# A graph network on one core: blocks of 2500 edges in the sorted last layer, layer norms with a bias on ScalarE, and loads moved into a prelude

## What is computed

```python
h = relu(layernorm(x));  x = x + gcn(h)         # msg = norm[row] * norm[col] * h[col], segment sum, @ W.T + b
h = relu(layernorm(x));  x = x + gat(h)         # 4 heads, softmax over each destination's edges
h = relu(layernorm(x));  x = x + weighted(h)    # two weighted steps: sum of x[src] * ew, mean, two matmuls, leaky relu
h = relu(layernorm(x))                          # last layer, edge-conditioned:
xw = h @ W                                      # 3125 x 128
ew = edge_attr @ edge_w                         # 103125 x 16 @ 16 x 128
msg = xw[src] * ew
out = segment_sum(msg, dst, num_segments=3125) + b
x = x + out
```

## Time and profile before

| | |
|---|---|
| median of three runs | 2925.09 us |
| profiled execution, its own time | 2937.53 us |
| its span, mean granted clock | 2935.8 us, 0.902 |
| PE / PEld busy | 2349.3 (80%) / 1710.9 (58%) |
| DVE / ACT / POOL busy | 1910.0 (65%) / 1408.7 (48%) / 1953.1 (67%) |
| hardware DMA queue | 171548 packets, 246.53 MB |
| software DMA queue (POOL's) | 48720 packets, 36.84 MB |

### The profile page before, as it was taken

The page is one execution under the profiler, slowest core; times in us unless marked ns, Lnnn a source line. Parts: engine busy times, 40 slices in busy tenths (PEclk is TensorE's granted clock), DMA queues, the critical chain, the costliest instruction groups (busy, mean ns, idle before and its releaser), DMA issues. The chain is left out here.

```text
span 2935.8 us, 64938 instructions
## 1 busy us (share of the span) xinstructions
PE 2349.3 (80%) x22192; PEld 1710.9 (58%) x22192; DVE 1910.0 (65%) x3810; ACT 1408.7 (48%) x2659; POOL 1953.1 (67%) x1608
## 2 busy tenths in 40 slices
PE   4677777766857777777788787889978999999998
PEld 2466666663424555555555555434546777777777
DVE  7999999983457777777777787211134555556555
ACT  0498988880038777777777775000003221222211
POOL 2278878805148888778777783577605888878874
PEclk7699999988968999988888899899987998999999
DMA  6267777768421111111111112996952222222213
GB/s 83 91 173 200 190 198 189 188 186 205 110 67 49 45 44 42 43 41 45 41 41 41 42 42 37 217 217 139 212 121 63 55 53 54 55 54 55 61 46 55
DMA packets 220459, 285.63 MB, mean 97 GB/s; under 512 B 130299, under 2 KB 166530, under 8 KB 217015
## 3 DMA queue, kind: packets, MB, share of 16 engines
q1 hardware_dynamic: 171548, 246.53, 33.8%
q0 software_dynamic: 48720, 36.84, 6.4%
HBM read 171.50 MB, written 112.09 MB: 97 GB/s over the span
## 5 line engine op out<-in xcount | busy, mean ns | idle before, releaser
L389 POOL DMA_INDIRECT scratch_slots<-sort_pay,sort_slot x400 | 590.0, 1475 | 185.2 <-issue 184.3
L1864 POOL TENSOR_TENSOR score<-score,rise 125x500 f32<-125x500 f32 (+1 forms) x609 | 671.9, 1139 | 52.5 <-DVE peaks L1800 48.5
L2399 POOL DMA_INDIRECT gathered_rows<-scratch_projected,src_i x425 | 532.4, 1253 | 156.7 <-issue 126.5
L1800 DVE CUSTOM_DVE_ANT_0 score<-raw,log_in 125x500 f32<-125x500 f32 (+1 forms) x609 | 353.9, 619 | 167.6 <-PE raw L1685 97.6
L1747 ACT ACTIVATE rise<-raw 125x1000 f32<-125x1000 f32 (+1 forms) x350 | 313.4, 918 | 183.1 <-DVE peaks L1800 95.7
L1700 PE MATMUL probsT<-ident,score 125*125 125x125 f32 x2175 | 363.8, 298 | 29.6 <-ACT score L1756 13.1
L1700 PEld LDWEIGHTS probsT<-ident,score 125*125 125x125 f32 x2175 | 304.3, 204 | 110.1 <-DVE weighed L1821 65.2
L874 PE MATMUL built<-pair_weight,hot 125*128 125x125 bf16 x3750 | 249.7, 229 | 63.9 <-DVE pair_weight L819 63.7
L1685 PE MATMUL raw<-QT,key 32*125 32x500 f32 (+1 forms) x1400 | 205.1, 657 | 94.8 <-DVE peaks L1800 90.8
L874 PEld LDWEIGHTS built<-pair_weight,hot 125*128 125x128 bf16 x3750 | 229.7, 103 | 75.8 <-DVE pair_weight L819 74.2
L1821 DVE COPY weighed<-probsT 125x500 f32<-125x500 f32 x400 | 251.1, 672 | 13.6 <-PE probsT L1700 13.6
(11 more groups left out here) (309 smaller groups left out, 4484.2 us busy)
## 6 DMA issues: line engine op xcount, KB each, us to landing
weights_in<-scratch_weightsT SPq DMA_DIRECT2D x50, 1093.8 KB
scratch_weightsT<-wT SPq DMA_DIRECT2D x25, 1367.2 KB
scratch_logs<-log SPq DMA_DIRECT2D x75, 437.5 KB
log_in<-scratch_logs SPq DMA_DIRECT2D x150, 218.8 KB
counts_in<-scratch_counts SPq DMA_DIRECT2D x25, 683.6 KB
scratch_counts<-cc SPq DMA_DIRECT2D x24, 683.6 KB
gathered_rows<-scratch_projected,src_i POOLq DMA_INDIRECT x425
scratch_slots<-sort_pay,sort_slot POOLq DMA_INDIRECT x400
```

The costliest lines, as they stand in the source:

```text
L389: nc.gpsimd.indirect_dma_start(rows, bass.IndirectOffsetOnAxis(ap=sort["slot"][:, b, c:c + 1], axis=0), pay[:, c, :], None).then_inc(sort[ ...
L1800: nc.vector.tensor_tensor_reduce(out=score[u][h][:, at:at + w], in0=raw[:, h, 0:w], in1=log_in[:, at:at + w], scale=1.0, scalar=-3e38, op0 ...
L1864: nc.gpsimd.tensor_tensor(score[u][h][:, at:at + w], score[u][h][:, at:at + w], rise[:, b, h, 0:w], ALU.add).then_inc(added, 1)
L2399: nc.gpsimd.indirect_dma_start(gathered[:, g % GATHERS, k, :], None, projected, bass.IndirectOffsetOnAxis(ap=src_i[:, FIRST + g, k:k + 1], ...
```

## The change

Blocks are half as long: 22 of 2500 edges, placed two at a time in 11 batches (five in adjacency, one in the first layer, five in weighted_layers). 55000 edges are sorted in place of 50000. 28 lists, each with one column of 128 slots; REACH is 88. A round takes four lists; 7 rounds per block, 154 in all, and 77 items, one in every second round. The turned slots stand as two halves in partitions 0 to 35 and 64 to 99, mix_attributes is two matmuls of 36 rows and 256 columns into two banks. The turned attributes share a bank of PSUM with the turned slots (tr_ps), with waits for each other's copies, and are turned ahead of sum_block. The slots have four buffers, filled by two DMAs per block; the first two blocks, the first attributes and the first three gathers are issued in the prelude. The rounding of list_rows runs one quad ahead, with three buffers; the bias goes to acc on POOL. The layer norm has relu(scale x X + lift) in one activation on ACT, with lift = -mean x scale from DVE. regular_gcn_layer hands its 15 semaphores on, so that one_over_degree clears 30.

```diff
-SORT_BLOCKS = 10
-COLS = 40
+BATCHES = 11
+PER_BATCH = 2
+SORT_BLOCKS = BATCHES * PER_BATCH
+COLS = 20
 BLOCK_EDGES = P * COLS
 SORTED = SORT_BLOCKS * BLOCK_EDGES
-LISTS = 26
+LISTS = 28
 DEPTH = (N + LISTS - 1) // LISTS
-SLOT_ROWS = 2 * FULL
 SLOT = EDIM + 2
-REACH = 168
+REACH = 88
+SECOND_ROWS = 64
+SLOT_ROWS_TURNED = SECOND_ROWS + 2 * SLOT
 GATHERED = SORTED // (EG * P)
 PLACED_IN_ADJACENCY = 5
...
-        for t in range(a, b):
-            nc.vector.tensor_scalar(H[:, t, :], X[:, t, :], mv[:, t, 0:1], 0.0, ALU.subtract, ALU.max)
         dve.wait_ge(std_ready, s + 1)
-        nc.vector.reciprocal(rstd[:, a:b], rstd[:, a:b]).then_inc(inv_ready, 1)
...
+        link(nc.vector.reciprocal(rstd[:, a:b], rstd[:, a:b]))
+        nc.vector.scalar_tensor_tensor(lift[:, a:b], mv[:, a:b, 0], -1.0, rstd[:, a:b], ALU.mult, ALU.mult).then_inc(inv_ready, 1)
...
-                    ins = nc.scalar.activation(H[:, t, :], H[:, t, :], ACT.Copy, scale=rstd[:, t:t + 1])
+                    ins = nc.scalar.activation(H[:, t, :], X[:, t, :], ACT.Relu, bias=lift[:, t:t + 1], scale=rstd[:, t:t + 1])
...
+def fetch_batch(nc, T, sort, b):
+
+    nc.gpsimd.dma_start(sort["raw"][:].rearrange("p (h n) -> p h n", h=PER_BATCH), attribute_batch(T, b)).then_inc(sort["raw_in"], 16)
...
-                    ins = nc.tensor.matmul(offset_ps[:], above16[:], in_list[:, :, :, c].rearrange("p b s -> p (b s)"),
-                                           start=(c == 0), stop=(c == COLS - 1))
+                    for u in range(2):
+                        ins = nc.tensor.matmul(offset_ps[:, u, 0:BATCHES * LISTS], above16[:],
+                                               in_list[:, BATCHES * u:BATCHES * (u + 1), :, c].rearrange("p b s -> p (b s)"),
+                                               start=(c == 0), stop=(c == COLS - 1))
...
-    PER_BLOCK = LISTS // 2
+    PER_BLOCK = LISTS // QUAD
+    BLOCK_BUFFERS = 4
+    HEAD_CHUNKS = 3
     ROUNDS = SORT_BLOCKS * PER_BLOCK
...
+            u = b % BLOCK_BUFFERS
+            by_half = slots[b].rearrange("r (j l x) w -> r j l (x w)", l=2, x=2)
+            for half in range(2):
+                at = half * SECOND_ROWS
+                sp.dma_start(pay[:, u, :, at:at + 2 * SLOT], by_half[:, :, half, :]).then_inc(slots_in[u], 16)
+
...
+                pool.wait_ge(emptied, 1)
+                nc.gpsimd.tensor_scalar(acc[:], acc[:], last["bias"][:, 0:1], None, ALU.add)
+                pool.wait_ge(stored, 32)
+                for k in range(HEAD_CHUNKS):
+                    gather_chunk(0, k)
...
+                load_block(sp, 0)
+                load_attributes(sp, 0)
+                load_block(sp, 1)
...
+
+                def round_rest(r):
+                    _, s0, n = fours[r]
+                    act.wait_ge(left, 2 * r if r else 1)
+                    nc.scalar.copy(table[:, s0:s0 + n, 1, :], rest[:, r % 3, 0:n, :]).then_inc(rounded, 1)
+
+                round_list(0)
+                for r in range(len(fours)):
+                    if r + 1 < len(fours):
+                        round_list(r + 1)
+                    round_rest(r)
...
-                dve.wait_ge(base_spread, 2)
-                nc.vector.tensor_tensor(X[:], X[:], bias[:].unsqueeze(1).broadcast_to([P, TILES, D]), ALU.add)
+                dve.wait_ge(base_spread, 1)
...
+                def reload_block(b):
+                    need(sp, s_turned, PER_BLOCK * (b - BLOCK_BUFFERS + 1))
+                    need(sp, s_goal, PER_BLOCK * (b - BLOCK_BUFFERS + 1))
+                    load_block(sp, b)
...
-                    sp.dma_start(attr[:, g % ATTRS, :], attributes[FIRST + g]).then_inc(attr_loaded[g % ATTRS], 16)
-                    while b < SORT_BLOCKS and (g - 1) * ROUNDS >= PER_BLOCK * (b - 1) * ITEMS:
-                        load_block(b)
+                    if g:
+                        load_attributes(sp, g)
+                    while b < SORT_BLOCKS and (g - 1) * ROUNDS >= PER_BLOCK * (b - BLOCK_BUFFERS + 1) * ITEMS:
+                        reload_block(b)
                         b += 1
...
+                    for k in range(HEAD_CHUNKS if g == 0 else 0, EG):
+                        gather_chunk(g, k)
...
-                    pe.wait_ge(slots_in[b % 2], 16 * (b // 2 + 1))
+                    pe.wait_ge(slots_in[b % BLOCK_BUFFERS], 32 * (b // BLOCK_BUFFERS + 1))
                     need(pe, s_kept, 2 * r)
-                    nc.tensor.transpose(tr_ps[:, 0:FULL], pay[:, b % 2, j * QROWS:(j + 1) * QROWS], ident[:]).then_inc(s_turned, 1)
+                    need(pe, kept, flats[0])
+                    nc.tensor.transpose(tr_ps[:, 0:FULL], pay[:, b % BLOCK_BUFFERS, j, 0:QROWS], ident[:]).then_inc(s_turned, 1)
+                    slots_turned[0] = r + 1
...
-                    nc.tensor.matmul(mixed_ps[:], pay_t[:, r % 2, :], quad_mix[:].rearrange("r c d -> r (c d)"), start=True,
-                                     stop=True).then_inc(s_mixed, 1)
+                    for half in range(2):
+                        rows = slice(half * SECOND_ROWS, half * SECOND_ROWS + 2 * SLOT)
+                        ins = nc.tensor.matmul(mixed_ps[:, half, 0:2 * D], pay_t[rows, r % 2, :],
+                                               quad_mix[rows].rearrange("r c d -> r (c d)"), start=True, stop=True)
+                    ins.then_inc(s_mixed, 1)
 
...
-                    nc.tensor.transpose(flat[:, 0:P], attr[:, g % ATTRS, :], ident[0:P, 0:P]).then_inc(turned, 1)
+                    need(pe, s_kept, 2 * slots_turned[0])
+                    flats[0] = g + 1
+                    nc.tensor.transpose(flat, attr[:, g % ATTRS, :], ident[0:P, 0:P]).then_inc(turned, 1)
...
                     if here(r):
                         get_rows(r)
+                    if r == -1:
+                        turn_attributes(0)
+                    if g is not None and g + 1 < ITEMS:
+                        turn_attributes(g + 1)
                     if here(r - 1):
                         sum_block(r - 1)
-                    if r == -1:
-                        turn_attributes(0)
                     if g is not None:
                         factors(g)
-                        if g + 1 < ITEMS:
-                            turn_attributes(g + 1)
```

More of the change, by code:

```diff
@@ L352, in _ @@
             sp.dma_start(table[ROWS:ROWS + GROWS, :], pad[:]).then_inc(table_done, 16)
-            with nc.allow_non_contiguous_dma(reason="runs of forty edges, and one destination of every block"):
+            with nc.allow_non_contiguous_dma(reason="runs of twenty edges, and one destination of every block"):
                 sp.dma_start(sort["base_i"][:], T["dst"][0:SORTED].rearrange("(o b r) -> o b r", o=1, r=BLOCK_EDGES)[:, :, 0]
@@ L388, in place_block, with place_batches @@
-    for c in range(COLS):
-        nc.gpsimd.indirect_dma_start(rows, bass.IndirectOffsetOnAxis(ap=sort["slot"][:, b, c:c + 1], axis=0), pay[:, c, :],
+        fetch_batch(nc, T, sort, b + 1)
+    rows = slots.rearrange("b r s w -> (b r s) w")
+    slot = of_batch(sort["slot"])
+    for c in range(PER_BATCH * COLS):
+        nc.gpsimd.indirect_dma_start(rows, bass.IndirectOffsetOnAxis(ap=slot[:, c:c + 1], axis=0), pay[:, c, :],
                                      None).then_inc(sort["placed"][u], 16)
-def place_blocks(nc, T, pool, sort, slots, first, end):
-    nc.gpsimd.dma_start(sort["raw"][:], attribute_block(T, first)).then_inc(sort["raw_in"], 16)
+def place_batches(nc, T, pool, sort, slots, first, end):
+    fetch_batch(nc, T, sort, first)
@@ L2086, in _, with general_edges @@
                             multiply_output(G - 1)
-def general_edges(nc, T, src_i, dst_i, dst_rel, attr, attrT, mix, index, gathered, message, acc, ident,
+def general_edges(nc, T, src_i, dst_i, dst_rel, attr, attrT, mix, index, gathered, message, acc, bias, ident,
                   iota, iota_tile, projected):
@@ L2590, in edge_layer @@
         with nc.If(nc.values_load(irregular[0:1, 0:1], min_val=0, max_val=1) != 0):
-            general_edges(nc, T, src_i, dst_i, dst_rel, attr, attrT, mix, index, gathered, message, acc, ident,
-                          iota, iota_tile, projected)
+            general_edges(nc, T, src_i, dst_i, dst_rel, attr, attrT, mix, index, gathered, message, acc, last["bias"],
+                          ident, iota, iota_tile, projected)
         with ExitStack() as c3:
```

237 lines of the change are left out of this document (128 added, 109 removed).

## The result

Measured beside the kernel before on the same chip, the changed kernel took 3104.14 us (median of four runs, 3083.93 to 3145.14) against 2930.23: the ratio is 1.056, 95% interval 1.045 to 1.066. The ratio is that of the fast runs and leaves out the one of 3145.14 us. It is slower by 5.6%, where 2845 us was predicted. The profiled execution has a span of 3114.1 us and a mean granted clock of 0.841. On four other chips the kernel before has medians of 2891 to 2895 us, and on two of them the changed kernel took 2828.85 (ratio 0.976, 0.969 to 0.983) and 2839.37 (0.981, 0.976 to 0.986). Both results are real, and most of what follows is about what stands between them.

The account below looks back on a forecast made before the run. POOL's gathers were to bound the changed main loop, PE close behind. The terms -83.8 - 3.2 - 6.4 + 5.3 + 1 + 7.1 = -80.0 took the median 2925.09 to 2845 us, range 2822 to 2890.

Parts of the forecast that it names:

- 6 us on the start: Main loop, PE: an estimated 6 us for the start at low clock, added to 550 to give 556.
- the 45 us of idle: Main loop before: PE idles about 45 us in the ring of factors and messages; a spare round would remove it.
- a clock under .94: Main loop, sign of being right: PE's mean clock is under .94 since it idles more.
- 608: Main loop time forecast: POOL's 598 us plus 10, that is -83.8.
- Rival A: Main loop: PE stays the bound, halves not overlapping or paying .16 per change; loop 621 to 660, time 2858 to 2897, chance .28.
- the forecast's 598 to 625: Main loop range of the main forecast: halves overlap and POOL bounds, time 2835 to 2862, chance .53.
- the forecast bound of 598: Main loop, POOL: 382 gathers at 1.550 us make 592, plus 6 behind the last one.
- 7.14: Main loop, PE: two rounds and one item take 7.14 us at full clock, 550 us for 77.
- Rivals B and C: Main loop: B, gathers slower, loop 655 at 1.70 us, chance .09; C, slots arrive late, loop 887 at .36, chance .04.
- Forecast -6.4: Layer norms of attention and the last: -3.2 us each from dropping DVE's subtract-and-max, together -6.4.
- +5.3: Edge slots: wider compare, multiply and offset matmuls less small operations add 5.3 us, bounds 0 and +8.
- +7.1: Weighted stage: a fifth placement batch on POOL ends after PE's matmuls, adding 7.1 us, bounds 0 and +9.

Follow-up runs that it names:

- The forced waits: Nine waits from idle DVE additions: kernel before 2926.02 us, changed 3006.01; changed with early messages 2968.77, also with one mix matmul 2908.38 or REACH 168 2907.36.
- early messages: Changed kernel with each item's message made one round earlier on DVE: 2820.01 us, ratio 0.975 to the kernel before.
- full mix kernel: Changed kernel with mix_attributes as one matmul of 100 rows and 512 columns: 2831.08 us, ratio 0.979 to the kernel before.
- second profile: Unedited kernels profiled again on other chips than the first: kernel before 2888.82 us, changed kernel 2828.85.
- the third: Changed kernel, unedited, a third time beside the kernel before: 2839.37 us, ratio 0.981.

## Why the prediction was wrong

**The clock.** The step that failed is the clock of the main loop. The prediction saw that it falls at waits, put 6 us on the start, let the 45 us of idle go, and with them put every other low round at nothing; that the clock would come back as fast as before, it took without a word. Its own edits took the way back away: narrower sums and half matmuls, costed as time saved, made 1 or 2 low rounds into up to 20. The forced waits show that both edits do this; that the first chip's waits are what sets it off there rests on its traces alone. It even forecast a clock under .94, but as a sign of idling; PE was busy. On the first chip that is 889 us for 608. Rival A's 660 was no bound either, and no rival had this mechanism; every round of the trace of before has 168 columns, so no row showed a loop of narrow passes at the low clock, and the prediction should have asked what the clock does there.

**The loop where nothing disturbs.** 623 and 627 us, at the top of the forecast's 598 to 625, but POOL did not bound: its last gather ends 30 us before DVE's last addition, where 6 were forecast. PE bound, with a price at the changes to and from halves, which is rival A's case. The start alone holds nine and ten low rounds where 6 us were allowed: 9 x 3.36 = 30 us. With early messages, and two low rounds, it is 597 beside the forecast bound of 598, though for another reason: a pair takes 7.62 and not 7.14, so PE needs 77 x 7.62 = 587 and bounds, with POOL's last gather 13 us before the last addition. Of the .48, spread is .09 longer per round and sum_edges .11 (1.14 for 1.03); sum_block takes .91 and .86 for .83; mix is .63 for .61, factors 1.12 for 1.08. In the full mix kernel spread is .22 and sum_edges 1.03 again, so a change between half and full matmuls has a price of about .1, and the halves in all save 7.88 - 7.62 = .26 a pair, 20 us and not 46. So the halves did overlap, and rival A's drain was there, with .1 for .16 and at three places of a pair for four. The Trainium skill, page "TensorEngine Tiling (Array Packing)", section "Key Properties", speaks of that drain without a price, and the trace agrees with it.

**Rivals B and C.** Gathers kept 1.51 us from start to start, and no engine waits for slots_in: both fell.

**Norms.** Forecast -6.4: in the kernel with the norm alone, the one ahead of attention gave under 1 (attention starts at 841.3 for 842.2) and the last 1.7 (18.1 to 16.4 us from its first statistic to its last turned row). "ACT's 25 activations stay" was wrong, for they got longer, which takes 25 x .09 = 2.3 us of each norm (source views of ACT, before and norm alone, ns):

```profile
L168 ACT ACTIVATE H<-H,rstd x100: 384/386/402, 76.7 to 2190.4; 125x128 f32<-125x128 f32 x100
...
L167 ACT ACTIVATE H<-X,lift,rstd x100: 477/478/493, 74.5 to 2143.4; 125x128 f32<-125x128 f32 x100
```

The -48 of the whole came for the most part with DVE's stops, which the prediction did not see.

**Outside the loop**, on the undisturbed chips: edge slots +4.4 (adjacency begins at 131.7 for 127.3) for +5.3. The sum is right and its parts are not: 40 matmuls of 308 columns took 22.04 us against 21.83 for 260, so the 40 matmuls took the same time with more columns at half the stride; whether a column got cheaper or something else sets the .55 us of each, no run separates. The Trainium skill, page "SBUF — State Buffer", section "Door 1: The DMA port swizzle (why `[64,N]` ≈ `[32,N]`)", with its lines of 16 bytes, would have left a column at its price, and the measurement does not bear that out. From there to attention's first score it took 5.5 and 4.3 us longer, for -2.2. From attention's end to the last product it took 371 and 374 for 365, +6 and +9, for which the prediction had nothing. Its +7.1 was for POOL's last placement ending after PE, and that came too: it ends 5.8 and 2.1 us after the last product starts, and the norm's first operation waits 7.1 and 3.5 us for .3 before. Before (second profile) and changed kernel:

```profile
2174.41 2.42 DVE L145 BATCH_NORM_STATS2 stats<-X 125x6 f32<-125x128 f32 x12 [0.32 <-PEq L1924]
...
2148.61 1.19 POOL L399 DMA_INDIRECT scratch_slots<-sort_pay,sort_slot  x1 [2.49 <-issue]
...
2151.83 2.42 DVE L148 BATCH_NORM_STATS2 stats<-X 125x6 f32<-125x128 f32 x12 [7.13 <-PEq L1942]
```

So the weighted stage cost about 13 in both, for +7.1. From the last product to the loop's first turn it took 50 and 46 for 49. Without that wait it is -6 in both, where 3.2 for the norm, 3.2 for the prelude and the slots' 3.4 were forecast; POOL's addition of the bias (8.44 us) and DVE's part of the lists fall together, as below. (The terms of the edge slots add up to 5.2 and those of the weighted stage to 7.0, not 5.3 and 7.1.)

**The total.** 2829 and 2839 on two chips are near 2845, but that is luck: the loop gave -35 and -31 and not -84, attention -45 and -39 where the prediction had nothing, and the other stages together +17 and +15 and not +3.8.

## What to carry to other kernels

When an edit makes matmuls narrower or uses half of the array, cost the loop at the low clock too, and see with a forced wait how long it stays there; then take out the waits that make the clock fall, since here one reordering on DVE (early message) made the clock 0.99 and the loop 597 us for 623; its 2820 us are the shortest time here, though only 9 under the changed kernel's on another chip, since its attention took 13 us longer. Forced waits of known length are a cheap test of how robust a kernel is, and they showed what one chip's profile could not. Before a gain is credited to an edit, look whether it lies where the edit is, and bring the instruction count back to what it was, to see if the gain stays.

## What the runs showed of the hardware

PE at 100% busy stayed at 1.2 GHz for 138 us. Engines of one chip idled up to 2.8 us for what the trace calls remote, those of four others never did in the loop. DVE stopped at ten fixed places of attention, for 4.6 to 5.2 us or for 2.6 to 3.0, by the number of its instructions ahead. And while POOL added the bias to 128 x 3213 elements, a DVE operation that takes .68 us took 2.35 and ended .27 after POOL's addition, while two others (L2370) ran at their .69 beside it (changed kernel, second profile; the third has 2.23 and .28):

```profile
2174.74 8.44 POOL L2293 TENSOR_SCALAR acc<-acc,last_bias 128x3213 f32<-128x3213 f32 x1
...
2181.10 2.35 DVE L2376 TENSOR_TENSOR list_rows<-rows_rest,list_rows 112x512 bf16<-112x512 f32 x1
2183.37 0.68 DVE L2370 TENSOR_TENSOR rows_rest<-strided,list_rows 112x512 f32<-112x512 f32 x1
```
